# Cross attention: when a quarter's maxima are taken, and in which order GpSimd splits them

## What is computed

```
qh, kh, vh = split_heads(layernorm(x) @ w_q + b_q), split_heads(ctx @ w_k + b_k), split_heads(ctx @ w_v + b_v)
scores = einsum('bhqd,bhkd->bhqk', qh, kh) / sqrt(8)
scores = where(mask, -1e9, scores)
x = x + tanh(g) * (einsum('bhqk,bhkd->bhqd', softmax(scores), vh) @ w_o + b_o)
```

## Time and profile before

| | us |
|---|---|
| three runs | 5996.71, 5977.54, 5991.94 (median 5991.94) |
| the profiled execution, its own time | 6002.82 |
| span of its trace | 6001.0 |
| cross attention, first and last start of the second pass's products (L759) | 105.6 to 2072.6 |
| busy over the span | PE 93%, PEld 55%, DVE 60%, ACT 68%, POOL 44% |

### The profile page before, as it was taken

One profiled execution on the slowest core, in us unless ns is written; L12 is line 12 of the kernel. 1 busy time (PEld: TensorE's weight loads), 2 busy tenths in 40 slices (PEclk: granted clock), 3 DMA queues, 4 the chain that ended last, 5 costly groups with the idle time before them and its releaser, 6 DMA issues.

```text
span 6001.0 us, 161497 instructions
## 1 busy us (share of the span) xinstructions
PE 5562.2 (93%) x51848; PEld 3310.2 (55%) x51848; DVE 3590.1 (60%) x7913; ACT 4052.7 (68%) x10886; POOL 2654.8 (44%) x2280
## 2 busy tenths in 40 slices
PE   5999999999999879999999999999998999999997
PEld 2444444444444356666666666666665666656665
DVE  3666666666666546655666566656665566556654
ACT  2555554555545467887878777877787778877885
POOL 2111221112211055655555555655565555655563
PEclk9999999999999989999999999999999999999998
DMA  3333233333334043233323333333333323333332
GB/s 79 68 73 62 56 69 64 74 59 58 67 65 74 14 134 98 89 95 108 100 92 92 102 104 94 92 96 108 94 92 97 106 94 92 93 111 93 92 93 74
DMA packets 146300, 512.29 MB, mean 85 GB/s; under 512 B 31996, under 2 KB 48252, under 8 KB 127404
## 3 DMA queue, kind: packets, MB, share of 16 engines
q1 hardware_dynamic: 144300, 506.02, 32.2%
q10 hardware_dynamic: 1536, 0.40, 0.0%
HBM read 223.41 MB, written 30.68 MB: 42 GB/s over the span
## 4 chain that ended last, share of the span: by engine, by line
PE 47%; ACT 9%; issue 4%; DVE 2%; DMA 1%; ACTq 0%; SPq 0%; POOL 0%; DVEq 0%; POOLq 0%
PE b_qk L1420 9%; PE b_c L1461 6%; PE b_o L1382 6%; PE b_pt L1363 5%; PE b_sc L1351 4%; PE b_nv L1398 3%; PE b_qk L1431 3%; PE b_nv L1451 2%; ACT probs L1131 2%; PE b_sc L1342 2%; PE b_c L1491 2%; ACT L78 1%; PE b_nv L1491 1%; ACT L1170 1%; DMA v<-v 1%
## 5 line engine op out<-in xcount | busy, mean ns | idle before, releaser
L441 ACT ACTIVATE eT<-b_e 128x512 f32<-128x512 f32 (+1 forms) x1664 | 907.6, 594 | 972.1 <-PE b_e L759 966.5
L1131 ACT ACTIVATE probs<-b_sc,nb,rq 128x96 f32<-128x96 f32 (+1 forms) x3072 | 1322.4, 449 | 41.1 <-DVE nb L1265 41.1
L514 DVE CUSTOM_DVE_ANT_0 junk<-b_s,mq 128x1024 bf16<-128x1024 f32 (+1 forms) x1024 | 1000.3, 991 | 436.8 <-PE b_s L741 412.2
L1062 POOL TENSOR_TENSOR probs<-probs,rsums 128x512 f32<-128x512 f32 (+1 forms) x768 | 716.4, 933 | 752.1 <-DVE rsums L1201 745.3
L1256 DVE TENSOR_REDUCE b_sc<-b_sc 128x4 f32<-128x512 f32 (+1 forms) x768 | 486.3, 633 | 878.0 <-PE b_sc L1351 877.7
L1121 ACT ACTIVATE probsT<-b_pt 128x512 f32<-128x512 f32 x768 | 457.5, 596 | 601.0 <-PE b_pt L1363 596.7
L1420 PE MATMUL b_qk<-xs,weights 128*128 128x256 f32 x3072 | 751.3, 389 | 87.7 <-POOL xs L1054 49.1
L755 PE MATMUL b_e<-mk,identb 128*128 128x512 bf16 (+1 forms) x1664 | 656.2, 394 | 54.2 <-DMA q_op<-mp 44.2
L1382 PEld LDWEIGHTS b_o<-probsT,v 128*64 128x64 f32 x9216 | 376.8, 138 | 572.6 <-issue 502.2
L1420 PEld LDWEIGHTS b_qk<-xs,weights 128*128 128x128 f32 x3072 | 562.8, 193 | 177.0 <-issue 64.5
L759 PE MATMUL b_e<-q_op,k_op 75*128 75x256 bf16 (+1 forms) x3328 | 659.3, 280 | 0.0
(11 more groups left out here) (132 smaller groups left out, 8344.9 us busy)
## 6 DMA issues: line engine op xcount, KB each, us to landing
rot_p<-rot_s SPq DMA_DIRECT2D x768, 256.0 KB, 2.4
rkb<-rk_scr SPq DMA_DIRECT2D x192, 512.0 KB, 5.9
k_op<-k_scr SPq DMA_DIRECT2D x576, 100.1 KB
v<-v SPq DMA_DIRECT2D x192, 256.0 KB, 3.6
k_scr<-kp SPq DMA_DIRECT2D x48, 400.2 KB, 3.5
ctxT<-in_ctx SPq DMA_DIRECT2D x17, 800.5 KB, 20.2
weights<-in_ffn_w SPq DMA_DIRECT2D x24, 512.0 KB, 5.3
q_op<-q_scr SPq DMA_DIRECT2D x144, 64.0 KB
```

Of the source, the lines that this page charges most:

```text
L441: nc.scalar.activation(eT[0:n, g % 2, i * 512:(i + 1) * 512], b_e[i][0:n, :], ACT.Exp).then_inc(s["e_ready"], 1)
L514: nc.vector.tensor_tensor_reduce(junk[:, half, 0:n], b_s[u % 2][:, 0:n], mq[:, p, qt, half * 1024:half * 1024 + n], 1.0, LOWEST, ALU.add, ...
L1062: nc.gpsimd.tensor_tensor(pu, pu, rsums[:, u % 2, :].unsqueeze(2).to_broadcast([P, 4, w]), ALU.mult).then_inc(s["pn_ready"], 1)
L1131: last = nc.scalar.activation(probs[:, t, k % 2, 2 * e + h, c0:P], b_sc[:, 512 * e + h * w:512 * e + (h + 1) * w], ACT.Exp, bias=nb[:, k % ...
```

## The change

The units for the maxima end at key step 5 in place of 7 (so groups begin at step 5 too), the split rows leave at step 8 in place of 10 (L474 has `TURN + 3` in place of 10), and on GpSimd `max_parts` of quarter 0 comes ahead of the first subtraction for the keys. The last two key jobs in `b_p` go from steps 5 and 6 to steps 6 and 7, `v` job 1 from (1, 5) to (1, 7), and the two roundings of the keys on ScalarE from steps 7 and 10 of quarter 0 to 8 and 11.

```
-TURN = 7
+TURN = 5
...
-                at += [(0, 3, "k", 0), (0, 4, "k", 1), (0, 5, "k", 2), (0, 6, "k", 3), (0, 9, "mean_q", 0),
-                       (0, 11, "var_q", 0), (1, 1, "q", 0), (1, 3, "v", 0), (1, 5, "v", 1), (1, 9, "v", 2),
+                at += [(0, 3, "k", 0), (0, 4, "k", 1), (0, 6, "k", 2), (0, 7, "k", 3), (0, 9, "mean_q", 0),
+                       (0, 11, "var_q", 0), (1, 1, "q", 0), (1, 3, "v", 0), (1, 7, "v", 1), (1, 9, "v", 2),
                        (1, 11, "v", 3), (3, TURN, "max", 3)]
...
-                    if nxt and q == 0:
-                        b = nxt[0]
-                        pool.wait_ge(s["khi_ready"], count("khi_ready", b, 1))
-                        nc.gpsimd.tensor_tensor(kf[:, :], kf[:, :], kp[:, 0, :], ALU.subtract
-                                                ).then_inc(s["kres_ready"], 1)
...
                         max_parts(row, q)
                     if nxt and q == 0:
                         b = nxt[0]
+                        pool.wait_ge(s["khi_ready"], count("khi_ready", b, 1))
+                        nc.gpsimd.tensor_tensor(kf[:, :], kf[:, :], kp[:, 0, :], ALU.subtract
+                                                ).then_inc(s["kres_ready"], 1)
...
-                        if nxt and at == (0, 7):
+                        if nxt and at == (0, 8):
...
-                        if nxt and at == (0, 10):
+                        if nxt and at == (0, 11):
...
-                        if kt == 10:
+                        if kt == TURN + 3:
```

More of the change, by code:

```diff
@@ L390, in iteration @@
                         max_parts(row, q)
+                    if nxt and q == 0:
+                        b = nxt[0]
+                        pool.wait_ge(s["khi_ready"], count("khi_ready", b, 1))
+                        nc.gpsimd.tensor_tensor(kf[:, :], kf[:, :], kp[:, 0, :], ALU.subtract
+                                                ).then_inc(s["kres_ready"], 1)
                     if nxt and q == 0:
```

## The result

The changed kernel takes **6006.61 us** in the median of 8 runs (6001.84 to 6012.1), the kernel before 5991.02 us beside it (8 runs). The ratio is 1.0029, 95% interval 1.0019 to 1.0040: slower, by 15.6 us in the medians, at the edge of what I said can be told from no change. The profiled execution took 6011.1 us (span 6009.3).

What follows compares the result with a forecast made beforehand. TensorE, busy 1638 of 1700 us, was taken as the bound, with time to gain only from its idle stretches and clock. Terms 13 + 36 + 6 + 17 - 38 = +34 us gave 6026 us, range 5955 to 6066.

Steps and rivals of the forecast that it cites:

- GpSimd and ScalarE in quarter 0 ... Nothing.: Quarter 0: early split maxima, keys' split a step later and ScalarE's rounding at step 8 were to cost nothing.
- the falls behind the wait for `mneg`: Quarter 0, third key job: clock falls to 1.2 GHz in 9 of 14 iterations, 4.0 us each, +36 us.
- my +49: Quarter 0's terms together: 13 us of new wait for `mneg` and 36 us of clock falls.
- The wait for `mneg` itself: Quarter 0, third key job, step 6: TensorE waits 1.3 us where it waited 0.39, 13 us in 14 iterations.
- Quarter 2: Split rows still land with SyncE's backlog; step 5 needs queries 10.3 us after their reload: +6 us, plus 17 for falls.
- The +17 for falls: Quarter 2: 6 of 14 clock falls at 3.2 us become 9 of 14 at 4.0.
- Quarter 3: Fewer waits for the split maxima and fewer falls behind them, 10 us left together: -38 us.
- Arbitration: Rival, DMA queues: split rows' delay counts from their own issue, so sending earlier lands them earlier; +44, 6036 us; chance 0.2.
- The other side: Rival: waits at (0, 6) and in quarter 2 too short for clock falls; -48 us, 5944; chance 0.13.
- The signs: Profile after: 14 `mneg` waits of 1.1 to 1.6 us, query waits at (2, 5), fewer quarter 3 waits, clock 0.95 or below.
- The sum: All quarters' terms together: +34 us, 6026 us against the median; the forecast's own chance 0.35.

Runs made afterwards that it cites:

- the halves: The changed kernel with one of ScalarE's two key roundings back: only the first, at (0, 7), 0.9980; only the second, at (0, 10), 1.0013 against the kernel before.
- the pair: The changed kernel with both ScalarE roundings back at (0, 7) and (0, 10), key jobs left as changed: ratio to the kernel before 0.9948.
- the table: Kernels sending rows earlier: kernel before with rows one step earlier, 0.9982; the change, 1.0029; it with both roundings back, 0.9948; with key jobs back too, 0.9927.
- the two versions with the roundings back: The changed kernel with both roundings back, 0.9948, and with the two key jobs back as well, 0.9927 and 0.9938 on another chip, against the kernel before.
- the second execution: Profiled execution of the changed kernel run again unaltered, on the chip of the single-rounding versions: ratio to the kernel before 1.0031.
- the late keys alone: The kernel before (TURN 7) with only GpSimd's new order and ScalarE's roundings at (0, 8) and (0, 11): ratio 1.0125.
- the miss: TURN 6, keys as before, context loaded late, queries' store and reload ahead of the first k_op load, held to (1, 10): ratio to the kernel before 1.0121.
- context later: The kernel before with SyncE's context and mask loads put behind the k_op load at the head of quarter 3: ratio 0.9953.

## Why the prediction was wrong

It gave the direction, and a size twice too large, for reasons of which only some hold.

- **Step that failed: "GpSimd and ScalarE in quarter 0 ... Nothing."** I asked only what waits for the keys' parts, and found cover for it. I did not ask what runs beside GpSimd's operations in their new place: `y` and `xq`, VectorE's two operations with both inputs in SBUF, wait for them. It cost 24.6 us of waits at (0, 10), 14.9 at (1, 1), and quarter 0's half-clock time rose from 17.0 to 28.5: the halves and the pair show 0.5%, 0.2% and 0.8%.
- **Term that was mis-sized: the falls behind the wait for `mneg`, +36 us.** Measured: none. In five runs of this order the wait is there 70 times, 1.35 to 1.37 us, with no fall behind any. I had put it nearer the branches, "because they lie in the same quarter"; the 12 waits up to 1.49 us that I had counted without a fall were the better guide here. They are no rule either: in the change, waits of 1.36 and 1.43 us at (2, 0) had a fall. The two errors have nearly the same size (24.6 us of waits and 11.5 more at the half clock, for my 36) and opposite signs, so quarter 0's +52.7 is near my +49 by luck.
- **The wait for `mneg` itself: right.** 1.35 for the 1.3 us worked out; 19.0 us in 14, where 5.1 stood before, is +13.9 for +13.
- **Quarter 2: half right.** The rows land with the backlog, as the table shows. The unit of item 7 that needs the queries began at 1045.76, 9.8 us after their reload at 1035.94, for the 10.3 I took:

```profile
1035.94 3.44 SPq L321 DMA_DIRECT2D q_op<-q_scr  x9
```

```profile
1045.76 0.60 PE L741 MATMUL b_s<-k_op,q_op 72*128 72x512 bf16 x2 [1.00 <-DMA q_op<-q_scr]
```

  The +17 for falls did not come in the first execution (11.9 us at the half clock for 22.2) and came in small part in the second (25.6). I had missed that TensorE comes to quarter 2 later against the loads: 14.2 to 14.4 us after the first of them in the two executions of the change (and 14.1 and 14.2 in the two versions with the roundings back), for 13.7 before, which shortens the wait for the maxima by as much. I haven't found what sets this.
- **Quarter 3: right in kind, too small.** -38 was forecast, -49.3 and -46.4 measured; I had left 4 us of waits and one or two falls in it, 10 us together; there were 2.3 us of waits and 0.5 at the half clock (4.0 and 1.1 in the second execution).
- **The rivals.** Arbitration is out for quarter 2: by it the rows would have landed earlier in all four kernels of the table that sent them earlier. So the plain rule of the Trainium skill that I weighed (DMA: Bandwidth & Descriptors, "Queues, rings and completion order"), turns between queues packet by packet, is not what these small DMAs show. The other side, "waits too short to bring the clock down", was right in its mechanism at (0, 6), and is what the change does once both roundings are back: 0.5% faster than before, where I had priced it at -48 us (0.8%).
- **The signs.** The waits at L686 (1.35 to 1.37 us), those for the queries (9, up to 1.57 us) and the fewer waits of quarter 3 came as I said. The clock did not: 0.97, where I had 0.95 or below.
- **The sum.** +34 us was forecast, +15.6 measured in the medians. The direction holds, for a reason I did not give. The profiled executions give +8.3 and, for the second, +40 in the spans against the same profile of before, which spread is quarter 2's falls, besides what lies outside these 14 iterations.

Not settled: what sets how many of the equal waits for `smax` have a fall behind them; and 3.6 us that quarter 1 also gains with `xq` back at 415 ns.

## What to carry to other kernels

When a change moves an operation of GpSimd, list what VectorE runs beside its new place, and mark those with both inputs in SBUF: each that starts beside it ends just behind it (0.28 us here). A total of busy time that grows with the same instructions is the sign of it. And where small transfers of one queue land at a moment that follows another queue's loads, send them earlier and look whether the landing moves, before anything is paid for leaving earlier.

## What the runs showed of the hardware

- A 128x256 operation with two SBUF inputs took 0.41 to 0.43 us alone and, begun beside an operation of GpSimd, ended 0.27 to 0.28 us after it in every iteration of every run: 0.44 us beside the end of a short one, up to 2.91 us beside the subtraction, 3.80 us where two stood back to back. A unit with one SBUF input beside the same operations stayed at 1.23 us.
- It goes the other way too: whichever of the two starts second waits. In the late keys alone, `y` begun 0.01 us before a small GpSimd operation kept its 0.42 us and that operation took 0.67 us in place of 0.39 (seven times); begun 0.06 to 0.08 us after it, `y` took 3.80 us (seven times). GpSimd's subtraction took 3.42 us in the kernel before, where it began 0.35 us before the end of VectorE's product of two SBUF tensors (L608), and 3.22 us in the change, where it did not. In the miss, the first small subtraction of `max_parts` took 1.07 to 1.09 us beside the same product, and 0.66 otherwise.
- TensorE's clock did not follow the length of a wait alone. Waits of 1.35 us for `mneg` (70), 1.20 for `smax` (14) and 0.96 to 1.09 for `xq` (56) had no fall to the 1.2 GHz level behind them, while waits of 1.36 and 1.43 us (the change) and 1.28 us (context later) for the split maxima at (2, 0) had one. Waits of 1.75 us, equal to 0.01 us and at the same step, had one 10, 9 and 4 times of 14 in three runs, the last where the wait for `xq` at (1, 1), after them, was gone. Branches of 0.74 to 0.90 us had one now and then.
- Three transfers of 2 KB on ScalarE's queue landed 2.9 to 3.0 us after they left where SyncE had issued nothing for 16 us or more (quarter 3, context later). Behind SyncE's nine loads and a store they were through when TensorE went on, 14.7 to 15.5 us after the first of these loads, whether they left 3.8 or 8.5 us after it.
